# The second layer norm's tokens whitened on VectorE behind its roots, instead of on GpSimd

## What is computed

```
x  = x + attention0(layernorm(x)) * silu(experts(layernorm(x)))
xn = layernorm(x)
s  = linear_attention(xn)
y  = xn
for l in range(2):                      # _L1_ffn_ref, DEPTH = 2
    y = y + local_attention(shift_token(y) @ wqkv[l]) @ wo[l]
    h = shift_token(y)
    h = (h - h.mean(-1)) / sqrt(h.var(-1) + 1e-5) * ln_g[l] + ln_b[l]   # the second layer norm
    a, g = split(h @ w1[l] + b1[l])
    y = y + (a * gelu(g)) @ w2[l] + b2[l]
x  = x + s * silu(y)
```

## Time and profile before

| what | value |
|---|---|
| median of 3 runs | 2200.93 us (2199.74 to 2202.37) |
| the profiled execution, device time | 2202.68 us |
| its span in the profile | 2200.9 us |
| PE busy | 1851.0 us, 84% |
| PEld busy | 1176.2 us, 53% |
| DVE busy | 1244.6 us, 57% |
| ACT busy | 1210.0 us, 55% |
| POOL busy | 808.9 us, 37% |
| mean granted clock of TensorE | 0.915 of full speed |

### The profile page before, as it was taken

How to read it: one execution, slowest core, us unless ns; L and a number is a source line. 1 busy time by engine, 2 the same in 40 slices (tenths; PEclk the granted TensorE clock), 3 DMA queues, 4 the chain that set the end, 5 groups by cost and what they waited for, 6 DMA issues and landing times.

```text
span 2200.9 us, 38284 instructions
## 1 busy us (share of the span) xinstructions
PE 1851.0 (84%) x12692; PEld 1176.2 (53%) x12692; DVE 1244.6 (57%) x4083; ACT 1210.0 (55%) x3559; POOL 808.9 (37%) x913
## 2 busy tenths in 40 slices
PE   6589989987999789987999789987999877887866
PEld 4368745654565456554565455553565455464554
DVE  4434547556755556546755556546755556757553
ACT  2444546655565565555656565555656654644642
POOL 2733235223632253313632244313633243635421
PEclk9789999997999989998999989998999987988978
DMA  8156400000000000000000000000000000000000
GB/s 235 38 163 208 158 13 6 6 1 1 6 1 15 1 1 6 15 1 1 6 1 15 1 1 6 16 1 1 6 1 11 1 6 1 1 6 1 1 1 10
DMA packets 49725, 53.49 MB, mean 24 GB/s; under 512 B 6386, under 2 KB 42236, under 8 KB 49532
## 3 DMA queue, kind: packets, MB, share of 16 engines
q0 software_dynamic: 7808, 27.79, 3.9%
q1 hardware_dynamic: 41724, 23.26, 3.7%
HBM read 41.60 MB, written 9.44 MB: 23 GB/s over the span
## 4 chain that ended last, share of the span: by engine, by line
PE 62%; DVE 13%; ACT 10%; issue 8%; POOL 6%; DMA 1%; SPq 0%; DVEq 0%; POOLq 0%; ACTq 0%
PE ps L586 5%; PE ps L648 5%; PE ps L722 5%; PE ps L606 4%; PE ps L545 4%; PE ps L565 4%; PE ps L630 3%; PE ps L620 3%; PE ps L731 3%; PE ps L777 2%; ACT p L866 2%; POOL h L306 2%; PE ps L555 2%; PE ps L768 2%; PE ps L770 2%
## 5 line engine op out<-in xcount | busy, mean ns | idle before, releaser
L1330 POOL COPY rdx<-rden 128x256 f32<-128x256 f32 x256 | 99.5, 418 | 661.5 <-DVE rden L1049 628.6
L1032 DVE CUSTOM_DVE_ANT_0 p<-ps,mask,nrq 128x128 f32<-128x128 f32 x512 | 149.0, 347 | 274.3 <-PE ps L574 273.3
L1032 DVE CUSTOM_DVE_ANT_0 p<-ps,mask 128x128 f32<-128x128 f32 (+1 forms) x512 | 152.3, 354 | 255.9 <-PE ps L578 239.6
L586 PE MATMUL ps<-ident,p 128*128 128x128 f32 x1280 | 225.4, 300 | 27.5 <-ACT p L866 24.9
L866 ACT ACTIVATE p<-p,nmax 128x128 f32<-128x128 f32 (+1 forms) x512 | 226.5, 442 | 0.0
L722 PE MATMUL ps<-wqkv,hT 128*128 128x512 f32 x384 | 195.3, 617 | 29.6 <-ACT big L945 28.2
L865 ACT ACTIVATE p<-p,nmax 128x128 f32<-128x128 f32 x512 | 200.5, 392 | 31.0 <-DVE nmax L1032 30.4
L880 ACT ACTIVATE pt<-ps 128x384 f32<-128x384 f32 (+1 forms) x256 | 111.9, 437 | 189.4 <-PE ps L586 184.3
L586 PEld LDWEIGHTS ps<-ident,p 128*128 128x128 f32 x1280 | 145.7, 149 | 107.9 <-issue 95.2
L1439 POOL TENSOR_TENSOR big<-big,rots 128x512 f32<-128x512 f32 x64 | 100.3, 1567 | 224.1 <-ACT big L945 224.1
L555 PE MATMUL ps<-ident,big 128*128 128x128 f32 x512 | 86.1, 307 | 111.6 <-DVE big L1225 73.4
(11 more groups left out here) (248 smaller groups left out, 4250.6 us busy)
## 6 DMA issues: line engine op xcount, KB each, us to landing
slots_in<-xn SPq DMA_DIRECT2D x1, 2560.0 KB, 14.2
v<-slots_in SPq DMA_DIRECT2D x20, 128.0 KB
slots_out<-v SPq DMA_DIRECT2D x20, 128.0 KB
big<-in_x SPq DMA_DIRECT2D x4, 512.0 KB, 6.1
x<-in_x SPq DMA_DIRECT2D x8, 256.0 KB, 3.4
out_x<-x SPq DMA_DIRECT2D x8, 256.0 KB, 2.3
wqkv<-in_wqkv SPq DMA_DIRECT2D x2, 768.0 KB
xn<-in_x SPq DMA_DIRECT2D x6, 256.0 KB, 3.2
```

The lines of the kernel that those rows point to most:

```text
L586: last = nc.tensor.transpose(bank[:, j * P:(j + 1) * P], c.p[:, u % 4, j * P:(j + 1) * P], c.ident[:, :])
L1032: last = V.tensor_tensor_reduce(out=c.p[:, u % 4, a:b], in0=bank[:, a:b], in1=mask, scale=scale, scalar=3e38, op0=ALU.add, op1=ALU.min, ac ...
```

## The change

In segment `ln2n` DVE no longer signals POOL; it issues the four whitening instructions itself, right behind the last root, and the last one raises `hn_ready`. POOL's `ln2n` is gone. Since `rstd_ready` is now raised by the first layer norm only, POOL's `ln1n` counts to `b + 1`. The instruction itself, its operands and its tile shapes are the same on both engines.

```diff
@@ vector
     def ln2n(b, l):
         inverse_root(nc, link, c)
-        dve.sem_inc(c.rstd_ready, 1)
+        for t in range(TILES):
+            last = whiten(V, c.h[:, t, :], c.h[:, t, :], c.mv, c.rstd, t)
+        last.then_inc(c.hn_ready, 1)
@@ gpsimd
     def ln1n(b):
-        pool.wait_ge(c.rstd_ready, plan.whitened[("ln1n", b)])
+        pool.wait_ge(c.rstd_ready, b + 1)
...
-    def ln2n(b, l):
-        pool.wait_ge(c.rstd_ready, plan.whitened[("ln2n", b, l)])
-        for t in range(TILES):
-            last = whiten(G, c.h[:, t, :], c.h[:, t, :], c.mv, c.rstd, t)
-        last.then_inc(c.hn_ready, 1)
```

More of the change, by code:

```diff
@@ L1454, in gpsimd @@
     stage = {"scatter": scatter, "wg": wg, "r": r, "xn": xn, "tables": tables, "lin": lin, "kv": kv, "qkv": qkv,
-             "kn": kn, "shift": shift, "cum": cum, "ln1n": ln1n, "ln2n": ln2n}
+             "kn": kn, "shift": shift, "cum": cum, "ln1n": ln1n}
     pool.memset(c.zero[:, 0, :], 0.0).then_inc(c.zero_ready, 1)
```

## The result

The changed kernel takes 2163.4 us (median of 4, 2159.9 to 2164.6) against 2201.7 us before: the ratio is 0.9825, with a 95% interval of 0.9808 to 0.9842. The forecast was 2150, the range 2132 to 2173. The time lies in the range, and the gain of 38 us is three quarters of the forecast one. It lies 1.4 us outside the forecast's own range (2140 to 2162) and nearer to the first rival, the direct gain alone, at 2167. The profiled execution has a span of 2162.2 us.

The account below looks back on a forecast made before the run. The prediction took PE's queue, waiting 16 times for GpSimd's whitening, as the bound. From 2202.7 us it took 33.8 direct gain and 17.7 clock, giving 2151.2 profiled, 2150 median; range 2132 to 2173 us.

Parts of the forecast that it names:

- the first rival: Only the direct gain: the 1.27 us pause still brings the clock down, half-clock stretches last as before; 2167 us, chance 0.22.
- What bounds the kernel: PE's queue sets the pace; its chain of waits passes 16 times through GpSimd whitening `h`, 67.2 us in all.
- Price of a whitening, distance root to `yT`: VectorE's four whitenings take 1.10 us per place; last root to `yT` falls from 3.43 to 1.28 us.
- Direct gain: PE's wait before `yT` shrinks by 2.15 us at 15 places and 1.54 at place 12: 33.8 us.
- It moves up by three microseconds, and nothing on PE waits for it now, so it earns nothing: GpSimd's linear attention product, right behind the whitening in its queue, starts earlier; costed at nothing.
- The rule on the port: VectorE whitening and a GpSimd instruction may block each other; as a rival 2226 us, slower, chance 0.02.
- Clock term: Less half clock behind the waits before `yT`: 15 us at places 2 to 10, 1 at odd places, 1.7 at place 12.
- The step on the even places: At places 2 to 10 a 1.27 us pause mostly keeps the clock up; three quarters of 20.2 us, 15 us.
- its signs of being wrong: Whitenings over 0.4 us apart, ACT waiting for line 1032, half clock behind places 2 to 10 as before, new PE pauses.
- VectorE's queue: Behind the whitening, masking comes 1.1 us later but still before ACT needs it; delay costed at nothing.
- the rival that was given 0.06: VectorE's queue becomes the bound behind the whitening and masking is late, losing 1.1 us at every place; 2185 us, chance 0.06.

Follow-up runs that it names:

- e1_hold: The changed kernel with one added wait: GpSimd issues nothing in its ln2n segment until VectorE has taken the roots and whitened; 2147.6 us.
- e5_product_first: The kernel before, GpSimd still whitening, but at even places 2 to 10 its linear attention product goes ahead of its wait for the roots; 2201.2 us.
- e9_hold_roots_only: The changed kernel with GpSimd held only until the last root, so its product runs beside VectorE's whitening; 2163.4 us.
- e7_no_whitening: The changed kernel with GpSimd held as well, and the second layer norm's whitening left out, so its result is wrong; 2121.3 us.

## Why the prediction was right, and where it was not

**What bounds the kernel**: right. The wait before `yT` sat on the path 16 times, and shortening it was paid in time at nearly every place.

**Price of a whitening, distance root to `yT`**: right. Forecast 1.10 us and 1.28 us, measured 1.12 and 1.30 us, because the duration came from the same instruction on the same engine in the same trace.

**Direct gain**: forecast 33.8 us, measured 28.8 (67.2 less 38.4). The step that failed is the one on GpSimd's product, "It moves up by three microseconds, and nothing on PE waits for it now, so it earns nothing". It earned nothing, but it cost: 0.74 us of roots at five places and, with two more products, 2.8 us of roots at place 12, of which 1.2 us came through to `yT`. In e1_hold, where the products are kept back, PE's wait for the whitening is 33.5 us in total; the forecast had left 33.4 (67.2 less 33.8).

**The rule on the port** was weighed wrongly. The rule that VectorE and GpSimd block each other whole was put aside because GpSimd "has nothing to do then" at most places. That was true of the trace of before for the very reason that the change removes: GpSimd was waiting for the roots. The earlier trace rows was no evidence against the rule in general either. It has GpSimd whitening, one input; the two-input product is what held VectorE up, by 0.74 us on a root (e5_product_first) and by 0.66 us over four whitenings (e9_hold_roots_only). As the Trainium skill, "SBUF — State Buffer", section "Who interferes with whom", puts it for two-port instructions, "the other **fully blocks**"; here the held instruction ends with the product, within 0.1 us.

The trace of the kernel before had shown it already. In the first layer norm of six blocks a GpSimd product falls on the same root instructions, and two of them take 0.97 us each instead of 0.17. VectorE's and GpSimd's timeline there:

```profile
524.44 2.04 POOL L1316 TENSOR_TENSOR big<-big,rr 128x512 f32<-128x512 f32 x2
...
524.53 0.97 DVE L282 TENSOR_SCALAR scratch<-scratch 128x4 int32<-128x4 int32 x1
525.54 0.96 DVE L283 TENSOR_SCALAR rstd<-scratch 128x4 int32<-128x4 int32 x1
```

**Clock term**: forecast 17.7 us, of which 15 at the even places by half clock staying away there, 1 at the odd ones and 1.7 at place 12. The step on the even places failed: the clock fell at all five, which the prediction had listed among its signs of being wrong. The pause was 2.03 us and not 1.27. The even places still gave 12.5 us (40.4 to 15.5), because the stretches were shorter. Nothing here shows why; a longer pause doesn't mean a longer stretch, since e5_product_first, with pauses of 4.16 us, had 25.1 us of them. That gain was luck. The odd places gave 3.9 us instead of 1. Place 12, where I took back 1.7 us, lost 1.7 (half clock 3.4 to 6.8 us), and the last four another 1.8. In all, half clock behind `yT` fell from 91.8 to 66.1 us, worth 12.9 us. The length of a pause alone doesn't settle it: 1.28 us kept the clock at three places of five in one execution, and 2.37 us at three of six.

**VectorE's queue**: at nothing, right at the odd and even places; at place 12 the rival that was given 0.06 came true. Given back there are 2.3 us of wait at line 722 and 1.7 us of half clock, less 0.4 us by which the wait before `yT` still fell, together about the 3.3 us seen. The wait at line 722 is VectorE's full queue. It is 2.65 us in the changed kernel, 2.50 in e1_hold, where the roots are undisturbed, and 0.83 in e7_no_whitening, where the whitening is gone as well: the larger part is the whitening itself. The rest goes with GpSimd's products, which hold up the roots or, with the hold, line 1222; it was not measured apart.

**The sum of the miss**: the profiled execution was forecast at 2151.2 us and took 2164.0, a miss of 12.8. The pages split it. The wait before `yT` fell by 28.8 us instead of 33.8, so 5.0 us are missing. PE's busy time fell by 16.3 us (1851.0 to 1834.7) against the 17.7 of the clock term, 1.4 us missing; the stretches behind `yT` account for 12.9 of it. The last 6.4 us are a term that the forecast had at nothing, new idle time of PE in other places. It is 2.3 us at line 722, at place 12, and 4.9 us at line 555, of which 2.0 are the collision ahead of place 14, less some small gains. The group of line 555 before and after:

```profile
L555 PE MATMUL ps<-ident,big 128*128 128x128 f32 x512 | 86.1, 307 | 111.6 <-DVE big L1225 73.4 <-POOL big L1316 18.1 <-ACT rT L842 15.6
```

```profile
L555 PE MATMUL ps<-ident,big 128*128 128x128 f32 x512 | 87.0, 310 | 116.5 <-DVE big L1227 73.3 <-POOL big L1318 19.7 <-ACT rT L842 16.5
```

The clock term thus came out near its size, but not by the way that was forecast. e1_hold, which keeps the products back, measures 2147.6 us; that it comes close to 2150 is in part luck too, since its clock fell at two of the five even places and kept up at two of the odd ones.

## What to carry to other kernels

An engine that waits is quiet, and its quiet can be what a neighbour's speed rests on: before freeing one, look at which of its instructions moves into the gap and what the neighbour does there, and look in the trace for other places where the two already meet. Here a wait put back on GpSimd, whose work is late for nothing, was worth 16 us, as much as two fifths of the whole change. Where an in-order queue waits for two to four microseconds again and again, price the clock behind the wait as well as the wait; and read a trace before a theory falls by a time, since the clock hid 4 us in e5_product_first.

## What was not expected of the hardware

A GpSimd `tensor_tensor` of 0.93 us held VectorE instructions on 128x4 elements for its whole length, 0.91 instead of 0.17 us, and one on 128x128 for 1.00 instead of 0.34. GpSimd's two-input instructions held one-input and two-input ones alike (lines 282, 283, 285, 286 and 306), all with their operands in SBUF. The maskings of line 1032, which read PSUM, were not held, nor were the sums of line 1197 on 128x360 (0.81 us at most beside such an instruction, 0.79 in the median). GpSimd's one-input `tensor_scalar` in the earlier trace rows held VectorE up by no more than 0.1 us per instruction.

e1_hold's runs spread by 0.7%, from 2142.7 to 2157.0 us, those of the kernel before by 0.1%, from 2199.8 to 2202.5. Its pauses of 1.28 us sometimes keep the clock and sometimes don't, which would explain it; no experiment tested that.
